# Causal attention with scores computed twice, by queries for the maxima and by keys for the exponentials

## The reference, cut to what matters

```python
Q, K, V = (heads(W_Q), heads(W_K), heads(W_V))       # 16 heads, D_HEAD = 16
scores = jnp.einsum('bhqd,bhkd->bhqk', Q, K) / D_HEAD ** 0.5 + causal
probs = jax.nn.softmax(scores, axis=-1)
out = jnp.einsum('bhqk,bhkd->bhqd', probs, V)         # then @ W_o, residual
hidden = relu(x @ wi.T + low-rank) ; out = hidden @ wo.T + low-rank
gate = softmax(out @ gate_w + gate_b); top 2 of 8 experts, each w1, gelu, w2, gelu, w3
```

## Time and profile before

| | us |
|---|---|
| median of 3 runs | 1509.88 (1509.63 to 1516.31) |
| profiled execution | 1507.66 |
| its span | 1506.1 |
| busy TensorE | 1359.4 (90%) |
| busy VectorE | 875.0 (58%) |
| busy ScalarE | 767.0 (51%) |
| busy GpSimd | 420.0 (28%) |
| mean granted TensorE clock | 0.955 |

### The profile page before, as it was taken

The page is one execution under the profiler, slowest core; times in us unless marked ns, Lnnn a source line. Parts: engine busy times, 40 slices in busy tenths (PEclk is TensorE's granted clock), DMA queues, the critical chain, the costliest instruction groups (busy, mean ns, idle before and its releaser), DMA issues.

```text
span 1506.1 us, 32247 instructions
## 1 busy us (share of the span) xinstructions
PE 1359.4 (90%) x10297; PEld 1053.1 (70%) x10298; DVE 875.0 (58%) x1945; ACT 767.0 (51%) x2003; POOL 420.0 (28%) x553
## 2 busy tenths in 40 slices
PE   5989999999989989999999988249899999999997
PEld 3556766766766766766766757238788888888886
DVE  3765665665665665665666662645455555555554
ACT  4776676665666665675666651013233333333332
POOL 2212211221221211211212210133344444444442
PEclk9799999999999999999999999559999999999999
DMA  6112222222222222222222220652624223342221
GB/s 221 64 66 97 76 82 98 78 96 82 78 95 83 77 81 93 77 86 98 78 80 77 79 72 29 271 225 36 247 42 145 42 42 88 101 148 40 38 40 13
DMA packets 50642, 137.85 MB, mean 92 GB/s; under 512 B 10514, under 2 KB 29586, under 8 KB 48882
## 3 DMA queue, kind: packets, MB, share of 16 engines
q0 software_dynamic: 28992, 68.35, 16.9%
q1 hardware_dynamic: 21554, 68.18, 12.3%
HBM read 86.03 MB, written 51.38 MB: 91 GB/s over the span
## 4 chain that ended last, share of the span: by engine, by line
PE 81%; DVE 5%; ACT 4%; issue 4%; DMA 4%; POOL 1%; SPq 0%; POOLq 0%; DVEq 0%; ACTq 0%
PE bank L665 66%; PE bank L831 9%; PE bank L924 4%; ACT probs L1092 3%; DVE nmax L1276 2%; PE bank L916 1%; DMA xg<-hrows,gid 1%; DMA w_rest<-in_w_all 1%; DMA wsplit<-w_rest 1%; POOL hit_v L1536 0%; PE bank L839 0%; ACT w_high L990 0%; DVE probs_t L1290 0%; POOL w_rest L1516 0%; PE bank L779 0%
## 5 line engine op out<-in xcount | busy, mean ns | idle before, releaser
L1092 ACT ACTIVATE probs<-bank,nmax 128x512 f32<-128x512 f32 (+3 forms) x512 | 266.0, 525 | 164.4 <-DVE nmax L1276 163.0
L1276 DVE TENSOR_REDUCE nmax<-bank 128x1 f32<-128x512 f32 (+3 forms) x512 | 227.3, 486 | 201.7 <-PE bank L665 201.3
L1128 ACT ACTIVATE g<-z 128x512 f32<-128x512 f32 x142 | 89.8, 632 | 281.3 <-DVE z L1466 270.0
L831 PE MATMUL bank<-id_f,probs 128*128 128x128 f32 x1280 | 203.1, 290 | 0.4 <-ACT probs_t L1100 0.4
L1516 POOL TENSOR_TENSOR w_rest<-w_rest,w_high 128x512 f32<-128x512 f32 x64 | 81.4, 1271 | 425.5 <-ACT w_high L990 425.5
L665 PE MATMUL bank<-wst,g1t_high 128*128 x568 | 186.0, 409 | 0.9 <-DVE g1t_low L1454 0.9
L831 PEld LDWEIGHTS bank<-id_f,probs 128*128 128x128 f32 x1280 | 137.8, 143 | 45.0 <-issue 24.2
L1558 POOL DMA_INDIRECT out<-y_sb,sid x71 | 114.3, 1610 | 149.7 <-PE bank L916 67.1
L1290 DVE COPY probs_t<-bank 128x128 f32<-128x128 f32 (+3 forms) x320 | 140.1, 454 | 12.6 <-PE bank L831 12.6
L1466 DVE TENSOR_TENSOR z<-bank,b_sb 128x512 f32<-128x512 f32 x142 | 98.2, 692 | 74.3 <-PE bank L665 63.2
L665 PEld LDWEIGHTS bank<-wst,g1t_high 128*128 128x128 f32 x568 | 102.5, 190 | 20.8 <-issue 1.1
(11 more groups left out here) (213 smaller groups left out, 2879.2 us busy)
## 6 DMA issues: line engine op xcount, KB each, us to landing
wst<-wsplit SPq DMA_DIRECT2D x8, 4096.0 KB, 12.6
w_rest<-in_w_all POOLq DMA_DIRECT2D x64, 256.0 KB, 3.1
wsplit<-w_high POOLq DMA_DIRECT2D x64, 256.0 KB, 2.3
wsplit<-w_rest POOLq DMA_DIRECT2D x64, 256.0 KB, 2.6
hrows<-h_sb SPq DMA_DIRECT2D x8, 528.0 KB, 3.0
x_in<-in_xT SPq DMA_DIRECT2D x8, 512.0 KB, 3.5
wb_raw<-in_lora_wb SPq DMA_DIRECT2D x8, 512.0 KB, 3.5
x_res<-in_xT SPq DMA_DIRECT2D x8, 512.0 KB, 4.5
```

The lines of the kernel that those rows point to most:

```text
L831: ins = nc.tensor.transpose(at(n, rd)[:, kb * P:(kb + 1) * P], probs[:, t % 4, kb * P:(kb + 1) * P], id_f[:, :])
L1092: taken(nc.scalar.activation(probs[:, s % 4, 0:(i + 1) * P], at(n, rd)[:, 0:(i + 1) * P], ACT.Exp, bias=nmax[:, s % 8:s % 8 + 1], accum_ou ...
L1128: nc.scalar.activation(g[:, :], z[:, :], ACT.Gelu).then_inc(s_g, 1)
L1276: V.tensor_reduce(nmax[:, s % 8:s % 8 + 1], at(n, rd)[:, 0:(s // HEADS + 1) * P], AX.X, ALU.max, negate=True).then_inc(s_max, 1)
```

## The change

Attention is ordered by pairs of heads instead of tiles of queries. For each of 8 pairs the scores are computed by queries as before, in three chunks (`SCORE_CHUNKS`: tile 3; tiles 2 and 0; tile 1), one a step, only for their maxima. VectorE splits the 8 negated maxima of each query row in a high and a low part (`mm_sb`), four products with `id_r` turn them into rows, and ScalarE (even pairs) or VectorE (odd) copies these into rows 32 and 33 of the pair's strips of `q_sb`, where `k_sb` holds ones (it gets them from `marks_sb`). Five steps after the first, the scores are computed again with keys as rows (`st`, chunks `KEY_CHUNKS`), now with the maximum subtracted by the product, and ScalarE's exponential writes straight to `probs_t`. Above the diagonal GpSimd writes zeros by selects (`allowed`), two for the first diagonal blocks and two for the others. `v_sb` holds 16 columns of ones beside each 16 of values, so that the values product gives the sums too; every six steps it takes four heads over all 512 queries. Two `nn` products with `swap_sb` bring sums to values' rows, VectorE takes the reciprocal over 512 columns and multiplies. The transposes of probabilities and of sums, their copies, the row sums of ScalarE go; there are 34 steps.

The turn's fillers are dealt by `FILL_COUNTS` (0 to 2 a step), `low_o` is cut in four pieces. The residual is loaded into `x1t` itself after the `x1` fillers. GpSimd's loop has for each pair: two selects, load of a piece, two selects, subtraction and stores; the casts stand on ScalarE at steps 9, 12, ..., 30.

```diff
-W_OPENING = (0, 10)
-W_STEPS = (2, 8, 14, 19, 23, 28)
-T_LAG, PV_LAG = 1, 2
-INV_LAG, RT_LAG, NORM_LAG = 1, 2, 3
+SCORE_CHUNKS = ((3,), (2, 0), (1,))
+KEY_CHUNKS = ((0,), (3, 1), (2,))
+M_LAG, ST_LAG, PV_LAG, NORM_LAG = 4, 5, 12, 20
+FILL_COUNTS = [2] * 5 + [1] * 7 + [0] + [1] * 5 + [0, 1, 0, 1, 1, 1, 0] + [2] * 5 + [0, 1, 0, 1]
+CAST_LAG = 9
+def work_at(step):
+    return (chunk_at(step), chunk_at(step - ST_LAG), every(step - M_LAG, CHUNKS, PAIRS),
+            every(step - PV_LAG, 2 * CHUNKS, QUADS), every(step - NORM_LAG, 4 * CHUNKS, KD))
...
                 elif what == "x1t":
                     if m == 0:
-                        pe.wait_ge(free[PV_BANK], rd.start(PV_BANK, 1))
+                        pe.wait_ge(s_ot, KD * (p + 1))
...
+                    if late is not None:
+                        g, u = late
+                        if u == 0:
+                            drained(pe, ("m", g), rd)
+                        for half in range(2):
+                            vacant(pe, ("st", g, u, half), rd)
+                        for c, (kb, cols) in enumerate(key_tiles(u)):
+                            for half in range(2):
+                                n, r = ("st", g, u, half), STRIP * half
+                                ins = mm(at(n, rd)[:, cols], k_sb[r:r + STRIP, g, kb * P:(kb + 1) * P],
+                                         q_sb[r:r + STRIP, g, kb * P:S], start=True, stop=True, skip_group_check=True)
+                                if c == len(KEY_CHUNKS[u]) - 1:
+                                    done(ins, n, rd)
+                    if m is not None:
+                        n = ("m", m)
+                        vacant(pe, n, rd)
+                        pe.wait_ge(s_msplit, b * PAIRS + m + 1)
+                        for i in range(TB):
+                            ins = mm(at(n, rd)[:, i * P:(i + 1) * P], mm_sb[:, 2 * i:2 * i + P], id_r[:, :],
+                                     start=True, stop=True)
                         done(ins, n, rd)
...
+                    if quad is not None:
+                        n = ("pv", quad)
+                        vacant(pe, n, rd, [("v", t2) for t2 in range(TB // 2)] if quad == 0 else ())
+                        pe.wait_ge(s_pmask, 2 * (b * PAIRS + 2 * (quad + 1)))
...
+                            taken(nc.scalar.activation(probs_t[:, (2 * g + half) % PT_SLOTS, S * u:S * u + width],
+                                                       at(n, rd)[:, 0:width], ACT.Exp), n, rd)
...
+                        nc.scalar.activation(ot_sb[:, quad // 2, :], at(n, rd)[:, :], ACT.Identity, scale=marks_sb[:, 1:2])
+                        taken(nc.scalar.activation(sums[:, :], at(n, rd)[:, :], ACT.Identity, scale=marks_sb[:, 2:3]),
                               n, rd)
...
+                    cast_of = every(step - CAST_LAG, CHUNKS, PAIRS)
+                    if cast_of is not None:
+                        cast(b, cast_of)
...
+                        n = ("nn", norm)
                         filled(dve, n, rd)
...
+                        taken(V.reciprocal(rt_sb[:, :], at(n, rd)[:, :]), n, rd)
+                        drained(dve, n, rd)
+                        V.tensor_tensor(ot_sb[:, norm, :], ot_sb[:, norm, :], rt_sb[:, :], ALU.mult).then_inc(s_ot, 1)
...
+            def allowed(rd, g, u, tiles):
+
+                drained(pool, ("st", g, u, 1), rd)
+                at_0, at_1 = (PT_AT[kb] // P for kb in tiles)
+                for half in range(2):
+                    blocks = probs_t[:, (2 * g + half) % PT_SLOTS, :].rearrange("p (n c) -> p n c", c=P)
+                    diag = blocks[:, at_0:at_1 + 1:at_1 - at_0, :]
+                    ins = nc.gpsimd.affine_select(diag, diag, [[0, 2], [1, P]], ALU.is_ge, 0.0, base=0,
+                                                  channel_multiplier=-1)
+                ins.then_inc(s_pmask, 1)
+
+            def load_piece(b, piece):
+                cols = slice(piece * W_PIECE, (piece + 1) * W_PIECE)
+                if b or piece:
+                    pool.wait_ge(s_wsplit, (b * W_PIECES + piece) * 32)
+                pool.dma_start(w_rest[:, :], w_all[b:b + 1, :, cols].rearrange("o p n -> (o p) n")).then_inc(s_wpiece, 16)
...
+            for b in range(B):
+                rd = Round(b)
+                for g in range(PAIRS):
+                    allowed(rd, g, 1, (0, 3))
+                    load_piece(b, g)
+                    allowed(rd, g, 2, (1, 2))
+                    split_piece(b, g)
```

More of the change, by code:

```diff
@@ L64 @@
 PV_BANK = 6
[L65 to L87 removed]
+PAIRS = HEADS // 2
@@ L558, in _ @@
             conds = [("cond", o) for o in range(KD)]
-            x1ts = [("x1t", o) for o in range(KD)]
             hs = [("h", TB - 1)]
@@ new lines, in turn @@
+                    if m is not None and m % 2 == 0:
+                        n = ("m", m)
+                        filled(act, n, rd)
+                        for half in range(2):
+                            rows = slice(STRIP * half + M_ROW, STRIP * half + M_ROW + 2)
+                            ins = nc.scalar.copy(q_sb[rows, m, :], at(n, rd)[rows, :])
+                        taken(ins, n, rd)
+                    for n_fill, piece in rd.fillers(step):
+                        take(rd, n_fill, piece)
```

415 lines of the change are left out of this document (211 added, 204 removed).

## The result

The changed kernel took 1668.71 us (median of four runs, 1666.21 to 1677.76) against 1512.78 of the kernel before in the same session (1509.63 to 1516.31). The ratio is 1.1041, with a 95% interval of 1.0986 to 1.1095: slower by a tenth. The forecast was 1642, within 1585 to 1735.

A forecast was written before the change was run, and what follows sets the result against it. TensorE bound the kernel before; after, the weight pieces' loop: 61.7 + 13.0 + 26.3 + 23.5 + 1.4 = 125.9 us a turn against 109.4. Seven turns +115.5, the first +16.4: 1507.7 + 132 = 1640, plus 2.2: 1642, range 1585 to 1735.

The forecast's parts named there:

- one bare round of the loop: Weight piece through the single `w_rest` and `w_high`, subtraction, stores, next load, cast: 9.45 us a piece, no overlap.
- intervals 0 to 1 and 4 to 5: Between casts where ScalarE drains a values product, held by selects behind stores, ahead of the cast: 11.95 us each.
- six intervals: From subtraction 0 to subtraction 6 of a turn: two of 11.95 and four of 9.45, together 61.7 us.
- last product, gate, sums: Turn's end after subtraction 6: drained last values product 10.15, gate 1.85, sums product 0.96, together 13.0 us.
- wait and opening: The turn's opening, 25.2 us before, plus 1.1 of stall as `x1t` waits for reciprocal and multiplication: 26.3 us.
- The reciprocal: On VectorE over 512 columns: 3.0 us, priced only as 1.1 us of stall for `x1t` in the opening.
- The first turn: Its steps, 79.8 us before the change, were to take 96.2 us: +16.4.
- The selects: GpSimd's masks of 256 columns, priced at 0.7 us each by scaling the two-input subtraction.
- (a): Clock rival: 25 us of each opening and early steps at half clock, 12.5 us more a turn: 1742 us, chance 0.15.
- (b): Rival: masks and drains lengthen no interval, the loop binds alone, 56.7 us for six intervals: 1602 us, chance 0.14.
- (c): Rival: GpSimd's selects take 2 us each, some 17 us more a turn: 1778 us, chance 0.06.
- (d): Rival: loop stays hidden, TensorE's shorter queue sets the pace, turn 102.6 us including 4 of maxima waits: 1454 us, chance 0.06.

The follow-up runs named there:

- packed_before: The kernel before with only its eight casts a turn moved to steps 9, 12, ..., 30: 1622.96 us, ratio 1.0726 to the kernel before.
- no_selects: The changed kernel without GpSimd's selects, the values product waiting for the exponentials instead: 1594.36 us, ratio 1.0547 to the kernel before.
- cast_first: The changed kernel with ScalarE's casts of steps 12 and 24 ahead of its two drains of the values product: 1628.07 us, ratio 1.0763 to the kernel before.
- spread_bank6_act_chunks: `spread` plus sums product in bank 6, all copies of turned maxima on ScalarE, middle reciprocal in four pieces: 1484.07 us, ratio 0.9811 to the kernel before.
- spread: The changed kernel with casts at opening entries 0 and 10 and after steps 1, 7, 12, 18, 23, 29, GpSimd's work moved to match: 1528.32 us, ratio 1.0098.
- spread_bank6: `spread` plus the product of the sums in bank 6, the values' bank, instead of a score bank: 1530.25 us, ratio 1.013 to the kernel before.

## Why the prediction was right, and by how much its steps were off

The main step held: the loop of a weight piece can't overlap itself, packed into 21 steps it is slower than TensorE, and TensorE's saving goes into waits. The casts wait for loads over 100 us, as the prediction's last part asked; 23 of the 32 values products are released by selects; the direction was right and 1668.7 lies 27 above the forecast of 1642 and inside the range. Taking the loop out gave 140 us back, and putting it into the old kernel cost 110. In the turn from 188.38 to 318.45, measured by subtractions as in the prediction:

| part of the turn, us | predicted | measured |
|---|---|---|
| one bare round of the loop | 9.45 | 8.64 |
| intervals 0 to 1 and 4 to 5 | 11.95 each | 10.8 and 14.9 |
| the other four together | 37.8 | 37.4 |
| six intervals | 61.7 | 63.1 |
| last product, gate, sums | 13.0 | 13.4 |
| wait and opening | 26.3 | 28.9 |
| steps 0 to 9 with the cast | 24.9 | 24.6 |
| turn | 125.9 | 130.1 |

**The round was too long by 0.8.** The timeline of GpSimd in the changed kernel:

```profile
329.20 1.27 POOL L1596 TENSOR_TENSOR w_rest<-w_rest,w_high 128x512 f32<-128x512 f32 x1 [4.42 <-ACT w_high L1025]
330.77 0.56 POOL L1600 DMA_DIRECT2D wsplit<-w_high  x1 [0.30 <-POOL w_rest L1596]
...
334.21 0.56 POOL L1590 DMA_DIRECT2D w_rest<-in_w_all  x1 [1.56 <-DMA wsplit<-w_rest]
...
337.83 1.29 POOL L1596 TENSOR_TENSOR w_rest<-w_rest,w_high 128x512 f32<-128x512 f32 x1 [2.28 <-ACT w_high L1025]
```

From subtraction to load are 5.01 us, against 5.61. Half of the difference is the gap between the subtraction's end and the first store's issue, 0.30 us here and 0.60 in the row of before, which is of the first turn (in the full turns it was 0.73); the rest is an earlier landing. The load lands after 2.9, not 3.1. I had taken the round of the kernel before as it stood, though GpSimd's program is another one; `packed_before` keeps the old one, with gaps of 0.73 in its full turns, and shows rounds of 9.5 to 9.9. With the measured 5.01 and the selects below, the sum for interval 0 to 1 is 10.7 instead of 11.95, and 10.8 are measured. Of this too long round little was seen in the total, and that is luck, because other things fill the intervals: a load that takes 3.97 us at 246.81, and a cast at 226.12 that stands behind late exponentials. In the same way the 13.0 for the last product, gate and sums came out at 13.4: the way from the subtraction to the product was 1.1 shorter (251.50 to 257.97), and the product took 4.24 us instead of 2.4 (257.97). The Trainium skill's formula (DMA: Bandwidth & Descriptors, "Anatomy of one DMA"), 2.6 us for such a piece, stands against 2.9 for the load and 2.3 to 2.6 for the stores: near, and nearer than the rows that I used.

**The reciprocal is the step that went wrong.** Its duration was forecast well, 3.0 from rows of 4 and 16 columns and 3.36 measured. Its place was not thought through. I priced it only for `x1t`, 1.1 us of stall a turn. It is in fact on two other paths. At the turn's end it holds a bank that the next `q` product needs: 3.7 us from the end of the sums product to 268.59, the table's 28.9, in place of 1.1; `x1t` itself waits for nothing more, and the opening after that takes the 25.2 it took before. In the middle of the turn it keeps the reductions back, TensorE waits 1.72 and 1.15 us, and the stretch behind, 229.28 to 239.86, runs at a clock of 0.59. The values product starts at 236.88 behind other products, while its selects had been done at 235.4. So interval 4 to 5 is 14.9 instead of 11.95, and 10.8 with a copy in place of the reciprocal. My list of what each instruction holds lacked the PSUM bank that it reads and the instructions behind it on VectorE, for this one alone.

**The first turn** was to bring 16.4 and brought 28.4. Cast 0 came at 53.44, within 1 us of the forecast. The last product ran at half the clock (126.51, 4.49 us for 2.4), and the steps end near 134.7 instead of 128.2; the `q` product then waits 3.54, and `q` and `k` take 4.7 us instead of 2.9. In sum, of the 27 us that the forecast fell short, 12 are the first turn's, 16 the seven full turns' (18.8 - 16.5 = 2.3 each). The full turns were further off than that. The 125.9 that was added up is 4.0 below the mean turn of 129.9; but the base from which it was counted, 109.4, is one turn, and the mean of the seven is 111.1. With that base the forecast would have been 1630, 12 us lower. That the forecast came this near is luck in part.

**The selects** took 0.414 us, two of them 0.77, where I took 0.7 for one. My figure came from the subtraction, which reads two inputs. The Trainium skill (GPSIMD Engine Reference, "Performance versus the Vector engine") led to an estimate of 0.2 to 0.4: the trace, just above the upper end of that estimate, is nearer to the page's simple loop than to my scaling. The error, some 0.6 for two selects, is small beside what a select waits for. By `no_selects` most of what they cost is their place in the queue, not their duration.

**The rivals.** (a) happened in part: mean clock 0.882. But the opening and steps 0 to 9, which it named, ran at 0.96 and 1.00 but for 4.5 us of `q` and `k` products at 0.61; the low stretches lie in steps 9 to 34, between the gaps, where the loop waits anyway, and where a product is on the chain they cost. The windows of the turn:

```profile
226.12:241.02 14.90, 12.13 (x80) 8.26 (x81) 7.25 (x14) 5.75 (x13) 4.46 (x8) 0.66 0.15 54
...
250.80:259.40 8.60, 1.65 (x9) 0.46 (x12) 1.00 (x2) 2.53 (x7) 4.46 (x8) 0.74 0.26 93
...
270.10:296.50 26.40, 25.62 (x133) 17.73 (x131) 17.54 (x29) 13.47 (x26) 0.00 (x0) 0.96 0.15 51
296.50:317.75 21.25, 19.45 (x123) 13.43 (x121) 15.17 (x37) 10.07 (x20) 2.03 (x5) 1.00 0.18 62
```

(b), the loop alone without long intervals, is out: `cast_first` shows that the drains cost, `no_selects` that the masks do. (c), slow selects, is out by their duration. (d), TensorE sets the pace and the turn falls to 102.6, is out for this kernel, and what it assumed doesn't hold even with the casts spread: TensorE's queue did become shorter (busy 660 of 740 us between 128 and 868, against 697 before, so 99.7 against 104.6 us a turn), and the turn stayed at 111.8. In that stretch the mean clock is 0.94 against 0.99, which makes the saving look smaller: in `spread_bank6_act_chunks`, at 0.98, it is 664 of 740, so 95.3 a turn and 9.3 less than before. The forecast of 7.5 lies between. In `spread` TensorE waits for VectorE: over the whole run 38.1 us for `rt_sb`, 21.3 for `q_sb`, 20.0 for `nmax`. When the middle reciprocal was cut the turn fell to 108.9, and when the copies went to ScalarE too, to 106.2, 4.9 below the old one. My price of 4 us for waits for maxima in (d) was too low.

What stays open: why other intervals became longer when the reciprocals became copies, and what the openings of the kernels with bank 6 would take if their second cast stood elsewhere. A second `w_rest` and `w_high`, which would let the loop overlap itself in the packed places, was not tried.

## What to carry to other kernels

A background loop with a single buffer has a shortest period that can be read off one round in the trace; compare it with the time between its places in the foreground's program before moving them, for where the foreground is quicker, an engine that runs in order hands the delay to everything behind. Look for the loop again after each gain elsewhere: here it came back in the opening once that had become shorter. For each long instruction that is put among short ones, list not only who needs its result but also the bank it holds and the instructions behind it on its engine; cutting it in pieces can pay even if the pieces take longer together. A saving on the busiest engine is worth what the others can follow: here the turn became 2.2 and then 4.9 us shorter than the old one only after VectorE had been relieved.

## What was unexpected of the hardware

- A wait of 2.9 us in a stretch that otherwise ran at full clock was followed by 8 us at 0.57, with TensorE busy for all of them, and then by 1.00 again. So the hole cost about twice its own length there. The same stretch without the hole had 1.00 throughout. One turn earlier it was alike: TensorE was busy 2.1 of the 5 us from 430 to 435, the next 5 had 0.50, the 5 behind them 0.99.
- A reciprocal of 512 columns from PSUM took 3.36 us on VectorE, and one of 128 columns 0.95; the multiplication that follows takes 0.69 when it runs alone. The price is by the column, some 6.3 ns, and cutting costs 4 x 0.95 - 3.36 = 0.4 us.
- The gap between the end of GpSimd's subtraction and the issue of the store that needs it was 0.60 us in the first turn and 0.73 or 0.74 in nearly all full turns of the kernel before, and the same in `packed_before`, which has the same program on GpSimd; it was 0.30 in the changed kernel, in `spread` and in `spread_bank6`, for the same two instructions. Why they differ was not tried.
